# A sorted-edge sweep whose destination ranges are 7, 9, 9 and 9 nodes wide and whose pages hold 19 columns

## The reference

```python
x = _layernorm(x + _L0_gnn_ref(x, ..., src, dst, edge_type_86), axis=-1)   # relational, 86 edge types
x = _layernorm(x + _L1_gnn_ref(x, edge_index, 3125), axis=-1)              # segment_sum(x[src], dst)
x = _layernorm(x + _L2_gnn_ref(x, L2_gnn_attn_w, src, dst), axis=-1)       # softmax attention over the edges
x = _layernorm(x + _L3_gnn_ref(x, src, dst), axis=-1)                      # 10 propagation steps
```

```python
x_hat = x[s] @ A1_w.T + A1_b
y_hat = x[d] @ A2_w.T + A2_b + rel_emb[t]
a     = tanh(relu(sum(x_hat * y_hat) / sqrt(32)))
nei   = segment_sum(a * sum_b(w_comp[t, b] * (x[s] @ weight[b])), dst)
h     = relu(nei + x[source of the last edge into d] @ self_loop_weight)
```

## Time and profile before

| what | us |
|---|---|
| median of 3 runs | 1105.08 |
| lowest and highest of the 3 | 1103.22, 1105.48 |
| the profiled execution: its own time | 1103.32 |
| the profiled execution: span from first to last instruction | 1101.1 |
| busy in it: PE, PEld | 902.0, 846.5 |
| busy in it: DVE, ACT, POOL | 942.5, 533.2, 579.0 |
| first and last L1400 of the sweep | 74.6, 754.8 |

### The profile page before, as it was taken

How to read it: one execution, slowest core, us unless ns; L and a number is a source line. 1 busy time by engine, 2 the same in 40 slices (tenths; PEclk the granted TensorE clock), 3 DMA queues, 4 the chain that set the end, 5 groups by cost and what they waited for, 6 DMA issues and landing times.

```text
span 1101.1 us, 57074 instructions
## 1 busy us (share of the span) xinstructions
PE 902.0 (82%) x24130; PEld 846.5 (77%) x24130; DVE 942.5 (86%) x2309; ACT 533.2 (48%) x1342; POOL 579.0 (53%) x546
## 2 busy tenths in 40 slices
PE   3338888988988988888888888885849958999996
PEld 3327778877877887778788778775749958999996
DVE  7959999999999999999999999996469976555556
ACT  1126565655656567767767767777675300000000
POOL 5777777777777777777777777772000000000000
PEclk9559998989989989989989989996869979999998
DMA  5253232323323333333333333320000000000001
GB/s 121 45 88 59 53 68 59 60 55 69 57 54 62 63 57 59 64 62 59 60 68 57 58 65 59 67 43 8 5 1 4 4 2 4 4 4 4 5 4 19
DMA packets 54401, 48.55 MB, mean 44 GB/s; under 512 B 35470, under 2 KB 44142, under 8 KB 54142
## 3 DMA queue, kind: packets, MB, share of 16 engines
q0 software_dynamic: 17088, 8.78, 10.6%
q10 hardware_dynamic: 11456, 22.01, 6.0%
q1 hardware_dynamic: 25598, 14.07, 5.5%
HBM read 42.49 MB, written 2.32 MB: 41 GB/s over the span
## 4 chain that ended last, share of the span: by engine, by line
DVE 51%; PE 33%; issue 7%; ACT 5%; DMA 3%; ACTq 0%; SPq 0%; DVEq 0%
PE ps L885 14%; DVE arena L1418 11%; DVE arena L1385 11%; PE ps L818 4%; PE ps L932 3%; DVE aggT L1431 3%; DVE arena L1439 3%; DVE arena L1400 2%; DVE arena L1412 2%; DVE arena L1404 2%; DVE arena L1375 2%; PE ps L916 2%; DVE arena L1362 2%; DVE arena L1448 2%; PE ps L856 2%
## 5 line engine op out<-in xcount | busy, mean ns | idle before, releaser
L632 POOL DMA_INDIRECT arena<-x_pad,arena x534 | 577.1, 1081 | 163.0 <-issue 162.4
L818 PE MATMUL ps<-aggT 128*128 128x128 f16 x3472 | 226.5, 229 | 0.0
L818 PEld LDWEIGHTS ps<-aggT 128*128 128x128 f16 x3472 | 215.8, 104 | 2.1 <-DVE aggT L1431 0.4
L1385 DVE TENSOR_SCALAR arena<-pair_no,arena 128x275 bf16<-128x275 f16 (+2 forms) x784 | 183.5, 287 | 0.0
L885 PE MATMUL ps<-arena,adj_words 128*128 128x64 f16 x5625 | 171.9, 192 | 3.4 <-DVEq L1703 3.2
L885 PEld LDWEIGHTS ps<-arena,adj_words 128*128 128x128 fp8e4 x5625 | 170.5, 97 | 4.7 <-DVEq L1703 3.6
L1418 DVE TENSOR_TENSOR arena<-ps,arena 128x1536 f32<-128x1536 f32 x98 | 171.3, 1748 | 0.2
L1080 ACT ACTIVATE adj_words<-arena 128x500 uint8 x196 | 126.6, 646 | 56.8 <-ACT arena L1055 56.0
L1050 ACT ACTIVATE arena<-ps 128x500 fp8e4<-128x500 f32 x196 | 114.3, 583 | 56.3 <-PE ps L767 34.4
L780 PE MATMUL ps<-arena 128*32 128x44 f32 (+3 forms) x7048 | 133.0, 211 | 5.4 <-DVE arena L1418 5.1
L780 PEld LDWEIGHTS ps<-arena 128*32 128x32 f32 x7048 | 109.0, 112 | 26.4 <-DVE arena L1418 8.2
(11 more groups left out here) (223 smaller groups left out, 1152.0 us busy)
## 6 DMA issues: line engine op xcount, KB each, us to landing
arena<-line_table ACTq DMA_DIRECT2D x48, 344.0 KB
arena<-x_pad,arena POOLq DMA_INDIRECT x534
arena<-pick_table SPq DMA_DIRECT2D x31, 256.0 KB
arena<-line_table ACTq DMA_DIRECT2D x48, 80.0 KB
arena<-dst_parts SPq DMA_DIRECT2D x196, 5.7 KB
agg_table<-arena SPq DMA_DIRECT2D x196, 2.5 KB
dst_parts<-aggT ACTq DMA_DIRECT2D x1, 735.0 KB, 11.4
x<-x_pad ACTq DMA_DIRECT2D x1, 400.0 KB, 13.7
```

The source lines that it names most:

```text
L632: pool.indirect_dma_start(to, None, table, bass.IndirectOffsetOnAxis(ap=index, axis=0)).then_inc(done, 16)
L818: mm = nc.tensor.matmul(ps[:, at:at + PICK_WIDE * FEAT], pick_hot[:, u % PICK_RING, k * P:(k + 1) * P], x_parts[:, t, j * PICK_WIDE:(j + 1 ...
L1385: last = v.tensor_scalar(pair_hot[:, d % 2, k, 0:n], pair_no[:, 0:n], pair_of[:, d * DUO + k // SLOTS, k % SLOTS:k % SLOTS + 1], None, ALU ...
```

## The change

Five constants. The ranges of tiles 0 to 3 start at 0, 2, 6 and 10 instead of 0, 1, 5 and 9; they are 7, 9, 9 and 9 nodes wide instead of 8, 11, 11 and 11; a page has 19 columns instead of 20.

```diff
-PAGE = 20
-STARTS = (0, 1, 5, 9)
-WIDTH = 11
+PAGE = 19
+STARTS = (0, 2, 6, 10)
+WIDTH = 9
 HOTS = WIDTH + 1
-PAIR_DSTS = (8, WIDTH, WIDTH, HOTS)
+PAIR_DSTS = (7, WIDTH, WIDTH, HOTS)
```

## The result

The changed kernel takes 1254.15 us (median of 4 runs, 1250.42 to 1256.3), the kernel before, in runs beside it, 1104.69. The ratio is 1.135 (95% interval 1.132 to 1.138). The profiled execution of the changed kernel has a span of 1253.2 us against 1101.1. The sweep's flag (L1495) is now written at 918 us instead of 766. From there to the end it is 335 us, as long as before, so the whole loss lies in the sweep.

What follows compares the result with a forecast made beforehand. The prediction took DVE's sweep and POOL's chain of gathers, ending with it, as two bounds at once. Gains of 1.3 + 1.8 + 1.4 = 4.5 us from the median of 1105.08 gave 1100.6 us, range 1089 to 1107.5.

Steps and rivals of the forecast that it cites:

- What the rest costs: PE counts, ACT passes, copies, number rows, memsets, dense stage and DMA pieces: each gives nothing by itself.
- The DVE saving: Shorter DVE instructions L1418, L1385, L1412 and L1366 in the sweep: together 39.7 us, 0.405 us of a duo.
- the other slope with the odd width: DVE's L1385: saving by the 0.20 ns slope if the odd 175 form carries 12 ns more: 5 us.
- The 39.7 us are then not paid out: Sweep: DVE runs free to about duo 37, then waits for POOL's gathers, some 2 us in each three duos.
- the slack at the end: End of sweep: L1400 of duo 97 stood at 754.76, its data was there by 753.50: 1.3 us gained.
- the tail: After duo 97's L1400, 11.8 us to the flag: column sum moved, L1418 and ACT's copies shorter: 1.4 us gained.
- POOL's pace: POOL's gathers in the sweep: lengthening beside DVE changes with DVE's share without PSUM operands: 1.8 us gained, 8 either side.
- POOL is freed: Rival: waiting DVE lets gathers take 1.25 us, POOL gains up to 42 us: 1064.0, half of it about 1084; chance 0.10.
- In step: Rival: DVE and POOL lock at a bad place, slower from 1.391 us a gather; 1117.3 at 1.43; chance 0.13.
- Doesn't do what it says: Rival: an edge lies outside its range and the general path runs, far slower; chance under 1%.
- Nothing that can be seen: Rival: POOL 2 to 6 us slower than summed, or no tail gain: 1102.9 to 1107.3 us; chance 0.19.
- the forecast's own case: Sweep: POOL as the bound, with a gain of 2.2 to 17 us; chance 0.58.

Runs made afterwards that it cites:

- rows20_all: Changed kernel with 20 rows instead of 19 in stores, dst_parts loads and the second half of line loads; engines still compute 19 columns: 1098.80 us.
- after_full: Changed kernel with each line load padded to 96 and 32 rows; stores and dst_parts loads stay at 19 rows: 1091.51 us.
- before_load: Kernel before with one more unused read of base_t into a SyncE register ahead of each of the 196 stores: 1144.68 us.
- rows20_full: Changed kernel with line loads padded to 96 and 32 rows, and 20 rows in stores and dst_parts loads: 1092.55 us.
- before_full: Kernel before with line loads padded to 96 and 32 rows; stores and dst_parts loads of 20 rows: 1103.76 us.

## Why the prediction was wrong, point by point

**The step that failed** is a sentence of "What the rest costs": "DMA pieces shrink by a twentieth: nothing." It priced a DMA by its bytes. Put right by rows20_all it is 155 us (1254.15 to 1098.80), the whole miss. The runs show that what counts is how many DMA engines the rows go to and what those engines carry already: with 19 rows everywhere but the line rows out of the way the loss is gone (after_full, 1091.51). The page's packet counts, 11456 and 25598, which the prediction didn't read, are more than its rows; asking what the others are leads there.

**What bounds the kernel** was incomplete. DVE and POOL were read rightly; SyncE wasn't read at all, and its 148.5 us of waits over 91 of 196 stores, with its 2.67 us of own work a group, made it the third bound (before_load). That made landings 0.8 us later time, where a queue with room to spare would have covered them.

**The DVE saving**: 39.7 us forecast; busy time fell from 942.5 to 903.9, 38.6. By form, of the changed kernel:

```profile
L1418 DVE TENSOR_TENSOR arena<-ps,arena 128x1280 f32<-128x1280 f32 x98 | 145.0, 1480 | 0.2
...
L1385 DVE TENSOR_SCALAR arena<-pair_no,arena 128x225 bf16<-128x225 f16 x392 | 102.2, 292 | 0.0
...
L1385 DVE TENSOR_SCALAR arena<-pair_no,arena 128x250 bf16<-128x250 f16 x196 | 57.3, 292 | 0.0
L1385 DVE TENSOR_SCALAR arena<-pair_no,arena 128x175 bf16<-128x175 f16 x196 | 53.0, 270 | 0.0
...
L1412 DVE TENSOR_TENSOR arena<-arena 128x160 f32<-128x160 f32 x98 | 31.3, 319 | 9.2 <-ACT arena L1101 9.2
L1366 DVE TENSOR_TENSOR arena<-next_no,arena 128x320 bf16<-128x320 bf16 x49 | 15.4, 314 | 0.0
```

L1418 at 1480 ns is exact (26.3 us for 26.1). L1412 gave 4.1 us for 3.1, L1366 1.7 for 1.6. L1385 gave 217.0 - 212.5 = 4.5 us, not 8.9: its forms take 270, 292 and 292 ns (262 to 284 was the sign), 250 elements as long as 225 and no less than 300, and 175 as long as 200 (269). Of the prediction's three sums for it, the 5 us of the other slope with the odd width came nearest.

**"The 39.7 us are then not paid out"** is right where it can be seen: rows20_full and after_full gain 11 to 12 us of 39. The wait was to begin about duo 37; in after_full the lead is 5.5 us there and 2.3 at duo 40. The idle time at the product is 26.3 us (20 to 40 said), the last gather ends at 744.7 (745 to 751 said), the leads of duos 91, 94 and 97 are 3.3, 3.1 and 2.4 us (1.5 to 5 said).

**The sum**, 4.5 us, held for the case without SyncE's trouble only in sign: 11.9 us between the medians, 10.2 between the profiles (1101.1 to 1090.9). By the prediction's own terms these 10.2 are: the slack at the end 0.8 us for 1.3 (from the last gather's end to the product 2.4 us, before 3.2); the tail from there to the flag 2.5 for 1.4 (9.3 us, before 11.8); POOL's pace 6.9 for 1.8, the term that was mis-sized. The gathers came at 1.373 us each over the run against 1.386, and since the first stands where it stood (12 us), the last one's end, 6.9 us earlier, is all pace. The padded loads don't explain it: in before_full, which has them too, the last gather ends at 755.2, 3.6 us later than in the kernel before, and in rows20_all, which doesn't, at 743.5. rows20_all, at 1098.80, lies within 2 us of the forecast 1100.6, but not for its reasons: there the lead of the gathers is still 10.3 us at duo 94 (2.7 in the kernel before), the product never waits, and DVE stands idle at the one-hots instead (32.1 us, 25.5 of them put down to nothing that the profile shows). A right number proves little about the mechanism.

**Rivals.** *POOL is freed*, up to 42 us: in after_full no more than the 6.9 us came of it. What an idle DVE gives POOL can be seen in the changed kernel, whose DVE is busy 75% of the stretch from 75 to 918 us, where it was busy 97% from 75 to 766: a gather takes 1030 ns instead of 1081, 27 us over 534. By the Trainium skill (SBUF — State Buffer, section on SBUF's two separate sides) DVE and GpSimd lock each other out of shared ports; the shorter gathers agree in direction. *In step*: didn't happen, 1.373 is under its limit of 1.391. *Doesn't do what it says*: no. *Nothing that can be seen*, 0.19: not so for the changed kernel, and after_full's 11.9 us are clear of it too. None of the four, and not the forecast's own case, said anything of DMA, and together they held all the chances.

## What to carry to other kernels

Before changing a dimension that a DMA carries as its row count, factor the old and the new number: 20 to 19 went from ten DMA engines to one, and padding 86 rows to 96 and 19 to 32 took the changed kernel from 1254.15 to 1091.51 us with a fifth more bytes. Then look at what else uses the same engines: a small move is late by what stands in front of it. And add up a queue that only issues DMAs and waits; its time is nowhere counted as busy, yet 2.7 us of instructions and 0.8 us of waiting a turn made it as much a bound as the engine that was busy 148.28 of 150 us.

## What the runs showed that I had not expected

- A 2.4 KB store lands in 1.3 us (median) on one DMA engine that no large load holds up (after_full), a 2.5 KB store on ten such engines in 1.5 (rows20_full). In the kernel before, where two engines carry the line rows, it takes 2.8: more engines are a gain only when they are free.
- The issue of a DMA of 6 rows holds ScalarE's queue 0.57 us, one of 80 rows 0.31, one of 86 rows 0.47 (medians).
- A read into a register on SyncE takes 0.50 us, and 0.27 when it stands right behind another one. 196 added reads cost the kernel 41 us.
- The kernel before left 344 KB of every line load to two DMA engines. Spreading it gave that kernel nothing (1103.76), and the changed one 163 us.
